# Four layers of a transformer on one core: attention ordered in cycles of two steps, value products first and projections behind them

## The reference

```python
Q = einsum('btd,hkd->bthk', x, W_Q) + b_Q       # K and V alike
scores = einsum('bqhk,bshk->bhqs', Q, K) / sqrt(64)
attn = softmax(scores, axis=-1)                 # layer 1: causal; layer 3: region mask and a bias per key
out_h = einsum('bhqs,bshk->bqhk', attn, V)
return einsum('bqhk,hdk->bqd', out_h, W_O) + b_O
```

## Time and profile before

| | us |
|---|---|
| median of 3 runs | 4065.98 (4064.16 to 4066.21) |
| the profiled execution | 4058.89 |
| its span, first to last instruction | 4056.9 |
| PE busy | 3683.7 (91%) |
| DVE busy | 2962.3 (73%) |
| ACT busy | 2270.1 (56%) |
| mean granted TensorE clock | 0.976 |

### The profile page before, as it was taken

One profiled execution on the slowest core, in us unless ns is written; L12 is line 12 of the kernel. 1 busy time (PEld: TensorE's weight loads), 2 busy tenths in 40 slices (PEclk: granted clock), 3 DMA queues, 4 the chain that ended last, 5 costly groups with the idle time before them and its releaser, 6 DMA issues.

```text
span 4056.9 us, 69226 instructions
## 1 busy us (share of the span) xinstructions
PE 3683.7 (91%) x25781; PEld 1829.9 (45%) x25781; DVE 2962.3 (73%) x5821; ACT 2270.1 (56%) x2635; POOL 11.1 (0%) x17
## 2 busy tenths in 40 slices
PE   4999999999999869888888896789999999999997
PEld 2444444444444335444444444334444444444444
DVE  6787787777878676666666666377787877878784
ACT  3666666666666415555455452466666656666663
POOL 1000000000000000000000000000000000000000
PEclk9999999999999989999999997899999999999998
DMA  1000000000000000000000000000000000000000
GB/s 54 7 9 9 9 11 7 10 9 9 9 7 9 14 1 9 15 12 15 9 15 10 13 12 6 13 9 11 8 11 7 11 10 7 11 7 9 7 9 16
DMA packets 44430, 44.66 MB, mean 11 GB/s; under 512 B 16466, under 2 KB 30554, under 8 KB 43834
## 3 DMA queue, kind: packets, MB, share of 16 engines
q1 hardware_dynamic: 44090, 40.09, 3.3%
HBM read 37.56 MB, written 1.70 MB: 10 GB/s over the span
## 4 chain that ended last, share of the span: by engine, by line
PE 70%; DVE 16%; issue 6%; ACT 6%; DMA 1%; SPq 1%; ACTq 0%; DVEq 0%
PE ps L565 66%; DVE acc L1190 4%; DVE over L1210 4%; ACT work L996 3%; DVE x L1341 1%; ACT over L1006 1%; PE ps L876 1%; PE ps L865 1%; DVE Kl L1133 1%; DVE stats L1106 1%; DVE oN L1168 1%; PE ps L554 1%; DVE mrow L1151 1%; PE ps L905 0%; DVE acc L1180 0%
## 5 line engine op out<-in xcount | busy, mean ns | idle before, releaser
L996 ACT ACTIVATE work<-ps 128x1024 f32<-128x1024 f32 (+1 forms) x1344 | 1265.6, 992 | 1205.2 <-PE ps L565 1205.2
L1190 DVE TENSOR_TENSOR acc<-acc,work 128x1024 f32<-128x1024 f32 (+2 forms) x1152 | 1361.2, 1182 | 327.4 <-ACT work L996 264.6
L565 PE MATMUL ps<-work,V 128*64 128x512 f32 (+3 forms) x5376 | 1263.0, 583 | 0.0
L565 PE MATMUL ps<-Qh,Kh 64*128 64x512 f32 (+3 forms) x2688 | 647.5, 477 | 8.8 <-issue 4.8
L1006 ACT ACTIVATE over<-ps 128x1024 f32<-128x1024 f32 x639 | 639.9, 1001 | 26.3 <-PE ps L565 25.8
L565 PEld LDWEIGHTS ps<-work,V 128*64 128x64 f32 x5376 | 398.4, 137 | 517.3 <-issue 453.2
L1210 DVE CUSTOM_DVE_ANT_0 over<-ps,over,mpart 128x512 f32<-128x512 f32 (+3 forms) x732 | 478.4, 690 | 188.6 <-PE ps L565 184.6
L565 PE MATMUL ps<-Qh,Kl 64*128 64x512 f32 (+3 forms) x2688 | 525.0, 386 | 0.0
L565 PE MATMUL ps<-Ql,Kh 64*128 64x512 f32 (+3 forms) x2688 | 519.9, 382 | 0.0
L565 PE MATMUL ps<-auxQ,auxK 64*128 64x512 bf16 (+3 forms) x2688 | 518.1, 380 | 0.0
L1210 DVE CUSTOM_DVE_ANT_0 over<-ps,over 128x512 f32<-128x512 f32 (+3 forms) x736 | 413.4, 600 | 132.1 <-PE ps L565 130.0
(11 more groups left out here) (186 smaller groups left out, 2239.0 us busy)
## 6 DMA issues: line engine op xcount, KB each, us to landing
rden<-inverse_sums SPq DMA_DIRECT2D x192, 128.0 KB, 2.9
auxQ<-mrow SPq DMA_DIRECT2D x384, 1.0 KB
wqk<-in_wqk SPq DMA_DIRECT2D x24, 128.0 KB, 2.3
dcomp<-den SPq DMA_DIRECT2D x192, 2.0 KB
wv<-in_wv SPq DMA_DIRECT2D x24, 64.0 KB, 2.2
inverse_sums<-rcomp SPq DMA_DIRECT2D x96, 4.0 KB, 1.3
work<-in_mlp_w SPq DMA_DIRECT2D x1, 1024.0 KB
work<-in_c_aux SPq DMA_DIRECT2D x1, 1024.0 KB, 4.7
```

Of the source, the lines that this page charges most:

```text
L565: return pe.matmul(o, w, m, start=start, stop=stop, skip_group_check=True)
L996: act.activation(work[:, 2 * e:2 * e + 2, q0:CH], ps[:, 2 * two:2 * two + 2, q0:CH], ACT.Exp, scale=L.scale).then_inc(s["p_ready"], 1)
L1190: dve.tensor_tensor(o, o, work[:, slots[two]:slots[two] + 2, q0:CH], ALU.add).then_inc(s["acc_ready"], 1)
```

## The change

Attention is ordered in cycles of two steps (G = K/2 a pair). PE runs a `row_block` and then a `column_block` a cycle; the loops are gone and every cycle is written out. The row block holds the base product of the first unit of the cycle before, four score tiles with the second unit's base between them, and the excess products of the cycle's two units. The column block holds the two value products of the cycle before, then the jobs of slots 0, 1 and 2, each slot with a bank of its own (MISC, and the two banks of odd score tiles). The second unit's excess goes to the banks of even score tiles, and its positive part to `over2`, which is the memory of the experts' weights; these are loaded after the first attention. The job tables are rewritten by cycle and slot. ScalarE and VectorE have a `cycle` each with the order shown. Scores, units, sums, values and jobs are the same in number and shape.

```diff
-MAXB, OUT, MISC = 4, 6, 7
+SCA, SCB, MAXB, OUT, MISC = 0, 2, 4, 6, 7
+SLOT_BANK = (MISC, SCB, SCB + 1)
...
-            qk_at, v_at = (0, 1, 5, 6, 11, 12, 16, 18), (5, 6, 11, 12)
-            mt_at, den_at, v_slot, wait = (-5, -3, 3, 10), (4, 8, 14, 21), 1, 3
+            qk_at = ((0, 1), (1, 2), (2, 1), (3, 2), (4, 0), (5, 2), (7, 0), (8, 2))
+            v_at = ((4, 1), (6, 2), (7, 1), (9, 0))
+            mt_at = ((-4, 0), (-2, 0), (1, 1), (5, 0))
+            den_at = ((2, 0), (5, 1), (8, 1), (10, 0))
+            op_at = ((4, 2), (7, 2), (10, 2), (12, 2))
         else:
             self.qk = [("K", 0), ("K", 1), ("K", 2), ("K", 3), ("Q", 0), ("Q", 1), ("Q", 2), ("Q", 3)]
-            qk_at, v_at = (0, 1, 3, 4, 5, 8, 9, 11), (12, 13, 16, 17)
-            mt_at, den_at, v_slot, wait = (-2, 6, 14, 22), (10, 18, 26, 34), 0, 4
-        op_at = [k + wait + 1 for k in den_at]
-        self.jobs = [(k - self.K, 0, kind, c) for k, (kind, c) in zip(qk_at, self.qk)]
-        self.jobs += [(k - self.K, v_slot, "V", c) for c, k in enumerate(v_at)]
-        self.jobs += [(k, 0, "mt", c) for c, k in enumerate(mt_at)]
-        self.jobs += [(k, 0, "den", c) for c, k in enumerate(den_at)]
-        self.jobs += [(k, 0, "op", c) for c, k in enumerate(op_at)]
+            qk_at = ((0, 1), (1, 0), (2, 1), (3, 1), (4, 1), (5, 0), (6, 1), (7, 1))
+            v_at = ((8, 1), (9, 0), (11, 1), (12, 1))
+            mt_at = ((-1, 0), (3, 0), (7, 0), (11, 0))
+            den_at = ((4, 0), (8, 0), (12, 0), (16, 0))
+            op_at = ((6, 0), (10, 0), (14, 0), (18, 0))
+        self.jobs = [(g - self.G, sl, kind, c) for (g, sl), (kind, c) in zip(qk_at, self.qk)]
+        self.jobs += [(g - self.G, sl, "V", c) for c, (g, sl) in enumerate(v_at)]
+        self.jobs += [(g, sl, "mt", c) for c, (g, sl) in enumerate(mt_at)]
+        self.jobs += [(g, sl, "den", c) for c, (g, sl) in enumerate(den_at)]
+        self.jobs += [(g, sl, "op", c) for c, (g, sl) in enumerate(op_at)]
...
+        self.mul_at = [(g + 2, c) for c, (g, _) in enumerate(den_at)]
+        self.inv_at = [(g + 1, c) for c, (g, _) in enumerate(den_at)]
+        self.out_at = [(k // 2, c) for c, k in enumerate(self.end)]
+        self.X = self.G * PAIRS + 3
...
-        den = sb("den", [P, CH])
...
+        den = rden
...
-        bT = [wexp[0:2 * TPC, p * NC:(p + 1) * NC, :] for p in range(2)]
+        bT = [wm[0:2 * TPC, p, :].rearrange("r (c q) -> r c q", q=P) for p in range(2)]
+        over2 = wexp[:].rearrange("p (m e) f -> p m (e f)", m=2)
...
-            return over if b == MAXB else work[:, 2 * RING - 2:2 * RING, :]
...
+            return over2 if slot else over
...
-                    for k in range(K):
-                        units = L.unit_here(k, main, prep)
...
+                def row_block(x):
+                    n, g = x // L.G, x % L.G
+                    p = n % 2
+                    tiles = 4 * x
+                    pending = {sl: (m, u) for sl, m, u in L.units_in(x - 1)}
+                    c = L.steps[2 * g][0]
+                    if 0 in pending:
+                        m, u = pending[0]
+                        base(m, m % 2, u)
+                    if g == 0:
+                        pe.wait_ge(s["lo_ready"], 8 * n + 8)
+                        if L.featured:
+                            pe.wait_ge(s["bias_in"], 64 * n + 64)
+                    if 2 * g == L.first[c]:
+                        pe.wait_ge(s["mrow_done"], 64 * (NC * n + c + 1))
+                    at_least(pe, s["p_ready"], tiles - 1)
+                    if 1 in pending:
+                        m, u = pending[1]
+                        pe.wait_ge(s["relu_ready"], L.NR * m + L.relus_to[u] + 1)
+                    scores(n, p, 2 * g, 0)
+                    at_least(pe, s["p_ready"], tiles)
+                    for b in SLOT_BANK[1:]:
+                        if job_at[b] is not None:
+                            released(*job_at[b])
+                            job_at[b] = None
+                    scores(n, p, 2 * g, 1)
+                    m0 = L.tile0_in(x)
+                    if m0 is not None:
+                        pe.wait_ge(s["bias_in"], 64 * m0 + 64)
+                        tile0(m0, m0 % 2)
+                        pe.wait_ge(s["p_ready"], tiles + 1)
+                        scores(n, p, 2 * g + 1, 0)
+                    if 1 in pending:
+                        m, u = pending[1]
+                        at_least(pe, s["top_ready"], L.NTOP * m + L.tops_to[u])
+                        base(m, m % 2, u)
+                    if m0 is None:
+                        pe.wait_ge(s["p_ready"], tiles + 1)
+                        scores(n, p, 2 * g + 1, 0)
+                    pe.wait_ge(s["p_ready"], tiles + 2)
+                    scores(n, p, 2 * g + 1, 1)
+                    units = L.units_in(x)
+                    for sl, m, u in units:
+                        if sl:
+                            pe.wait_ge(s["p_ready"], tiles + 3)
+                        at_least(pe, s["top_ready"], L.NTOP * units[0][1] + L.tops_to[units[0][2]])
+                        excess(m, m % 2, u, SCA if sl else MAXB)
+                def column_block(x):
+                    def jobs(slot):
+                        for sl, kind, m, c in L.jobs_in(x):
                             if sl == slot:
+                                b = SLOT_BANK[sl]
+                                if sl and L.main(x):
+                                    pe.wait_ge(s["p_ready"], 4 * x + 4)
+                                if job_at[b] is not None:
+                                    released(*job_at[b])
+                                job(kind, m, c, m % 2, b)
+                                job_at[b] = (kind, m, c)
+                    for half in range(2):
+                        if 0 < x <= L.G * PAIRS:
+                            n, g = (x - 1) // L.G, (x - 1) % L.G
+                            values(n, n % 2, 2 * g + half)
+                    for slot in range(3):
+                        jobs(slot)
...
-                each_stage(pe.Fori, opening, stage)
...
+                for at in range(L.X):
+                    if L.main(at):
+                        row_block(at)
+                    column_block(at)
...
+                def cycle(x):
+                    n, g = x // L.G, x % L.G
+                    def jobs(slot):
+                        for sl, kind, m, c in L.jobs_in(x):
+                            if sl == slot:
+                                job(kind, m, c, m % 2, SLOT_BANK[sl])
+                    if L.main(x):
+                        for j in range(4):
+                            tile = 4 * x + j
+                            q0 = L.steps[2 * g + j // 2][1][j % 2][1]
+                            e = tile % RING
+                            act.wait_ge(s["st_ready"], tile + 1)
+                            if tile >= RING:
+                                m, k = (tile - RING) // (2 * K), (tile - RING) % (2 * K) // 2
+                                act.wait_ge(s["acc_ready"], L.NS * m + L.sums_to[k + 1])
+                                act.wait_ge(s["pv_done"], (tile - RING) // 2 + 1)
+                            b = SCB if j % 2 else SCA
+                            act.activation(work[:, 2 * e:2 * e + 2, q0:CH], ps[:, b:b + 2, q0:CH], ACT.Exp,
+                                           scale=L.scale).then_inc(s["p_ready"], 1)
+                    for slot in range(2):
+                        for sl, m, u in L.units_in(x):
+                            if sl == slot:
                                 w = L.units[u][-1][2] + L.units[u][-1][4] * P
+                                b = SCA if sl else MAXB
+                                act.wait_ge(s["md_ready"], L.NR * m + L.relus_to[u] + 1)
+                                act.activation(excess_of(sl)[:, :, 0:w], ps[:, b:b + 2, 0:w], ACT.Relu)\
+                                    .then_inc(s["relu_ready"], 1)
+                        jobs(slot)
+                    for m, c in L.due(L.out_at, x):
+                        copy_out(m, c)
+                    jobs(2)
...
+                def cycle(x):
+                    before_ = L.units_in(x - 1)
+                    sums = sums_of(x) if L.main(x) else []
+                    last = sums_of(x - 1)[-1:] if 0 < x and L.main(x - 1) else []
+                    def jobs(slot):
+                        for sl, kind, m, c in L.jobs_in(x):
+                            if sl == slot:
+                                job(kind, m, c, m % 2, SLOT_BANK[sl])
+                    for sl, m, u in before_:
+                        if sl == 0:
+                            tops(m, u)
+                    for which in last:
+                        add(*which)
+                    if L.tile0_in(x) is not None:
+                        tops(L.tile0_in(x), 0)
+                    for sl, m, u in before_:
+                        if sl == 1:
+                            tops(m, u, slot=1)
```

(66 more changed lines are left out.)

223 lines of the change are left out of this document (61 added, 162 removed).

## The result

| | us |
|---|---|
| before, median of 4 runs | 4065.07 (4061.02 to 4066.21) |
| changed, median of 4 runs | 4661.97 (4653.62 to 4664.45) |
| ratio, 95% interval | 1.1467 (1.1447 to 1.1487) |
| predicted | 4610 (4430 to 4760) |

A forecast was written before the change was run, and what follows sets the result against it. PE's order was taken to bound attention, with VectorE's in-order queue making it wait. Span 4056.9 + 279 (layer 0) + 278 (layer 2) - 12 (layer 1) = 4602, execution 4604, median 4611, stated as 4610 us; range 4430 to 4760.

The forecast's parts named there:

- The bound and the rule: Attention: PE's order sets the time; VectorE's queue is in order, so PE pays for what stands ahead of a reduction.
- A cycle with nothing late: Attention cycle without late work: 9.08 us against 9.02 for two steps, saved tiling changes given back to exponentials in a row.
- the walk: Forecast's block-by-block timing of a pair's cycles: 202.5 us a pair in layer 0, 35.8 more than before.
- The tail behind a projection: Projection ending a block: its copy, Kl, Kd and a sum delay VectorE's first reduction; for K in slot 1, to 4.73 us.
- A + 3.12: Row block's end when late, 3.12 us after A, the end of VectorE's first reduction; 5.40 where nothing is late.
- Row maxima: Chunk's first scores wait for the row maxima's DMAs: 3.65 us from first issue to last landing, between 3.3 and 4.6.
- The clock: PE's clock: the main forecast counted no fall; a rival priced falls behind waits for row maxima at +109 us.
- rival D: Waits for row maxima drop PE's clock to 1.2 GHz, four times a pair in 16 pairs: +109 us, 4720; chance 0.14.
- A: Main forecast as walked: queued work behind late jobs makes PE wait; 4610 us, chance 0.67.
- Layer 1: Layer 1 attention: a pair 118.5 us against 121.2, about -12 us in all; only chunk 3 has "mt" right ahead of scores.
- The loops: Removing the loops over pairs in attention: little or nothing, since their pairs are in the means used.
- Rival B: VectorE's tail doesn't reach PE and saved tiling changes count: 154.6 us a pair, 3830 (about 4000 with exponentials' stalls); chance 0.06.

The follow-up runs named there:

- e2: Changed kernel with all of VectorE's sums but the left-over one ahead of a cycle's jobs, PE's order kept: 4416.83 us, ratio 1.0859.
- e7: Changed kernel with slot 0 and 1 jobs ahead of and between values, VectorE's sums ahead of jobs (behind row maxima), ScalarE's positive parts ahead of copies: 3910.03 us.
- e8: Changed kernel with 14 unread products ahead of PE's wait for the row maxima in the non-causal layers: 4580.36 us, ratio 1.1276.
- e1: Changed kernel with slot 0's job ahead of the value products and slot 1's between them on PE only: 3924.61 us, ratio 0.9643.
- e5: Kernel before the change with its loops over pairs 2 to 5 on PE and ScalarE written out: 4032.05 us, ratio 0.9929.
- e3: Changed kernel with the transposition of the row maxima in slot 0 ahead of the value products on PE: 4404.64 us, ratio 1.0827.

## Why the prediction was right, point by point

**The bound and the rule.** "What stands ahead of a reduction is paid by PE" held: e2 moves nothing but VectorE's sums and takes 245 us off. The row of 1.04 us of PE's idle behind three small instructions and a "mul" had shown it, where VectorE's busy share of 79% had not.

**A cycle with nothing late.** Forecast 9.08 us. Cycle 13 of the pair, from exponential to exponential:

```profile
654.78 1.95 ACT L1014 ACTIVATE work<-ps 128x1024 f32<-128x1024 f32 x2 [0.40 <-PE ps L558]
...
662.51 0.39 PE L558 MATMUL ps<-Qh,Kh 64*128 64x512 f32 x2
...
663.64 1.94 ACT L1014 ACTIVATE work<-ps 128x1024 f32<-128x1024 f32 x2 [2.75 <-PE ps L558]
...
664.31 0.50 PE L558 MATMUL ps<-Kh,Qh 64*128 64x512 f32 x2
```

8.86: 0.22 less. Two score tiles take 1.80 us (662.51 to 664.31) and not 1.84, and the first exponential starts 1.13 behind its scores and not 1.26; the rest of the difference wasn't followed up. If it held in all 16 cycles, the walk had 3.5 us a pair too much by it. That the change of tiling saved goes to exponentials in a row holds in part: in e7 a base product is followed by the next scores' weights only after

```profile
608.73 0.55 PE L558 MATMUL ps<-Kh,Qh 64*128 64x512 f32 x2
609.25 0.19 PEld L558 LDWEIGHTS ps<-Qh,Kh 64*128 64x128 f32 x2 [0.33 <-ACT work L1014]
```

0.52 us and not 0.23, released by ScalarE. With at most 0.37 saved, about 0.3 goes back here.

**The tail behind a projection.** The walk's end of the row block (A + 3.12) and the measured periods agree to 0.7 us: from first exponential to first exponential, cycles 5, 6, 7, 9 and 10 of pair 2 take 11.9, 12.2, 16.0, 11.3 and 9.8 us; the walk gives 12.6, 12.8, 16.1, 11.4 and 10.0 (row block, 3.68, the products of the jobs, and the shift of the first scores from one cycle to the next). The walk is the longer one in all five. Taken block by block over pairs 1 to 6 of layer 0, wherever no stretch at the lower clock falls into the block (for the first scores of a pair and of its third chunk, where one always does, e8's blocks stand in), a pair comes to about 196.6 us: the walk of 202.5 was 5.9 too long, 4.8 of it in the row blocks.

**Row maxima.** 3.61 us for 3.65. The landing time was an estimate between two bounds and sits at the near one.

**The clock.** The forecast put it at nothing. This was rival D with a chance of 0.14, and it came in, beside A. The windows of pairs 1 to 6 of layer 0, changed kernel and then e1 (length, busy time of PE, PEld, DVE, ACT, POOL, then clock):

```profile
281.50:1509.30 1227.80, 1037.05 (x6482) 506.27 (x6481) 769.36 (x1344) 626.79 (x697) 0.00 (x0) 0.95 0.02 7
244.30:1220.70 976.40, 966.70 (x6482) 490.64 (x6481) 771.48 (x1345) 621.68 (x696) 0.00 (x0) 1.00 0.03 9
```

The same 6482 products keep PE busy for 70 us more in six pairs, 11.7 a pair. Not all of this is loss, since PE would have waited in some of that time. Cycles behind a chunk's first scores take 0.7 to 1.4 us longer than the walk (cycle 4: 12.6 for 11.4; cycle 12: 12.4 for 11.4), there are others behind the waits for VectorE, and e8 gives 82 us for the part of it that was filled. From the 196.6 us above to the measured 204.6, the clock costs about 8 us a pair; over 16 pairs that is some 125 us, an estimate from layer 0. D was priced at 109. The walk's 5.9 us too much a pair and the clock's 8 nearly cancel. That 202.5 stands so near to 204.6, and 4610 to 4662, is in part luck.

**Layer 1.** The step that failed: -12 us forecast, +9 measured (122.6 a pair for 121.2, and 119.0 in e5, which has no loops either). Its slot 2 was taken as safe since no sum but one stands behind it; the first reduction and the sums behind slots 0 and 1 still stood there: e2 gives 7.6 us a pair in layer 1 and e3 5.1, where the walk had seen only one "mt" of 3.4. The forecast's own terms don't give its -12 either: they sum to 118.2 a pair and not 118.5, and eight pairs at 2.7 less would be -22.

**Sum.** From first to last exponential, layer 0 went from 1307 to 1596 us (+289 for 279 forecast), layer 1 from 931 to 940 (+9 for -12), layer 2 from 1320 to 1609 (+290 for 278): 588 for 545. The span grew by 602 (4056.9 to 4658.9), so 14 lie outside the attentions; the gating products of the experts, at the lower clock, are part of it (`ps<-wg,yT` takes 6.96 us at a clock of 0.50, before 4.41 at 0.82). The loops, put at little or nothing, are worth 33 us (e5): against a layer 0 without loops a pair lost 39.7 us and not 37.9. The load of the experts' weights is issued at 1693 and its first product starts at 1726, released by VectorE: hidden, as forecast.

**Rival B** failed as the change stands. But its terms are there once the queues fit: e7 is what it described, at 3910 and not 3830. Its pair of 154.6 us in layer 0 was 6.9 below e7's 161.5, 0.43 a cycle: that is about the 0.13 or more by which two changes are cheaper than 0.50, and the 0.3 given back to the exponentials.

## What to carry to other kernels

When work is moved on one engine, walk the queue of every other engine that consumes it, to the next instruction for which the first one waits: what stood beside 1.7 us of value products was free, and behind them cost 737 us (e1). Put the operation with the longest way back (a transposition whose result returns by DMA) first in a block and the one that nobody waits for last; in the consumers' queues, work that is ready goes ahead of work that isn't. Price a saved change of tiling (at most 0.37 us for two here) against the waits that the bunching makes.

## What the runs showed of the hardware

- The granted clock fell to 1.2 GHz behind PE waits of 1.5 and 3.2 us in layers where the kernel before held 2.4 GHz with a wait of 1.04 us in a step; 14 products that nothing reads, in the longer wait, made the kernel 82 us faster. With the longer waits nearly gone (e3, 8.7 us left of 181.2) it still fell at times: the mean is 0.98 in layer 0 and 0.96 in layer 2.
- A small product in the other tiling costs 0.37 us (0.32 to 0.39) more than one without a change of tiling (0.07). About 0.10 of it is the row product's own, so two changes cost 0.25 to 0.37 us.
- Loops over two pairs on two engines cost 33 us in three attentions, two passes each: the mean pair of layer 0 went from 166.7 to 164.9 us without them, that of layer 1 from 121.2 to 119.0.
